# The value products of two attention stages and the steps up to their transposes, one slot later

## Reference

```
x = LN(x + window_attention(x))            # 16 heads of 8, window 16, token 0 attends to all
x = LN(x + causal_attention(x) + cross_attention(x, ctx))   # one output projection for the sum
x = LN(x + expert_choice_ffn(x))
x = LN(x + gated_recurrence_and_mlp(x))
x = LN(x + cross_attention(x, ctx))
x = LN(x + top2_of_8_experts(x))
```

## Time and profile before

| what | value |
|---|---|
| median of 3 runs | 590.47 us |
| profiled execution | 588.99 us |
| its span, first to last instruction | 587.3 us |
| around the span | 1.7 us |
| granted TensorE clock, mean | 0.946 |
| PE busy, share | 478.7 us, 82% |
| DVE busy, share | 381.4 us, 65% |
| ACT busy, share | 222.9 us, 38% |
| POOL busy, share | 181.0 us, 31% |

### The profile page before, as it was taken

How to read it: one execution, slowest core, us unless ns; L and a number is a source line. 1 busy time by engine, 2 the same in 40 slices (tenths; PEclk the granted TensorE clock), 3 DMA queues, 4 the chain that set the end, 5 groups by cost and what they waited for, 6 DMA issues and landing times. The chain is left out here.

```text
span 587.3 us, 10442 instructions
## 1 busy us (share of the span) xinstructions
PE 478.7 (82%) x3790; PEld 233.6 (40%) x3837; DVE 381.4 (65%) x876; ACT 222.9 (38%) x449; POOL 181.0 (31%) x296
## 2 busy tenths in 40 slices
PE   3899999978879889875079994697599888999994
PEld 2445444433334333332037992246333333444441
DVE  7454766877667686515996557954458875466474
ACT  2303444454746646651002102432202666724221
POOL 6651639457363370406200004300142400000000
PEclk9899999999989999997589997989599999999998
DMA  7230103055411120006212004000031200060700
GB/s 233 67 81 27 47 2 103 19 172 173 138 55 27 49 56 4 3 1 226 98 53 93 3 2 160 1 2 1 26 89 48 57 3 3 33 184 1 215 19 18
DMA packets 26899, 38.03 MB, mean 65 GB/s; under 512 B 3648, under 2 KB 19520, under 8 KB 26464
## 3 DMA queue, kind: packets, MB, share of 16 engines
q1 hardware_dynamic: 26848, 37.36, 21.0%
HBM read 23.91 MB, written 0.59 MB: 42 GB/s over the span
## 5 line engine op out<-in xcount | busy, mean ns | idle before, releaser
L1070 DVE TENSOR_REDUCE nmax<-bank 128x2 f32<-128x512 f32 (+2 forms) x240 | 144.9, 625 | 79.8 <-PE bank L844 34.1
L956 ACT ACTIVATE arena<-bank 128x512 f32<-128x512 f32 (+2 forms) x256 | 130.7, 526 | 121.7 <-PE bank L848 84.4
L502 PE MATMUL bank<-causal_qk,identb 128*128 128x512 bf16 x255 | 80.8, 418 | 33.6 <-DVE moe_top L1350 16.0
L844 PE MATMUL bank<-arena 62*128 62x256 bf16 (+2 forms) x512 | 86.0, 257 | 12.9 <-DVE nmax L1070 5.3
L848 PE MATMUL bank<-arena 64*128 64x256 bf16 (+2 forms) x512 | 85.6, 256 | 2.2 <-ACT arena L956 1.5
L889 PE MATMUL bank<-arena 128*32 128x256 f32 (+4 forms) x1088 | 72.8, 346 | 8.6 <-ACT arena L956 3.7
L844 PEld LDWEIGHTS bank<-arena 62*128 62x128 bf16 x512 | 29.9, 94 | 79.3 <-issue 46.0
L502 PEld LDWEIGHTS bank<-causal_qk,identb 128*128 128x128 bf16 x298 | 26.4, 105 | 68.4 <-issue 40.0
L714 POOL TENSOR_SCALAR_AFFINE_SELECT arena<-arena 128x256 f32<-128x256 f32 x64 | 25.5, 407 | 48.6 <-ACT arena L956 47.8
L848 PEld LDWEIGHTS bank<-arena 64*128 64x128 bf16 x512 | 30.3, 94 | 16.5 <-issue 6.9
L889 PEld LDWEIGHTS bank<-arena 128*32 128x32 f32 x1088 | 21.4, 109 | 33.7 <-issue 18.6
(11 more groups left out here) (284 smaller groups left out, 794.5 us busy)
## 6 DMA issues: line engine op xcount, KB each, us to landing
arena<-arena SPq DMA_DIRECT2D x96, 128.0 KB, 2.4
fcw<-in_fc1T SPq DMA_DIRECT2D x16, 256.0 KB, 3.3
arena<-in_fc2T SPq DMA_DIRECT2D x1, 4096.0 KB, 14.9
arena<-comb_rows SPq DMA_DIRECT2D x16, 256.0 KB, 4.7
fcw<-in_last SPq DMA_DIRECT2D x1, 2304.0 KB, 8.3
arena<-pos_rows SPq DMA_DIRECT2D x16, 128.0 KB, 3.0
arena<-comb_rows SPq DMA_DIRECT2D x16, 128.0 KB, 4.5
w<-in_w SPq DMA_DIRECT2D x1, 1216.0 KB, 6.1
```

What stands on the lines that cost most here:

```text
L502: nc.tensor.matmul(bank[:, :], m.identb[:, :], m.causal_qk[:, 0:4, :], start=True, stop=True)
L844: mins = t.matmul(mout[:, i, :], stack_rows(m, nm, h0 + i, 0, MAX_ROWS)[:, qt * P:(qt + 1) * P], stack_rows(m, nm, h0 + i, 1, MAX_ROWS)[:, ...
L956: s.activation(m.prob[h % 8][:, 0:w], score_bank(n, h)[:, 0:w], ACT.Exp).then_inc(exps, 1)
L1070: v.tensor_reduce(m.nmax[n % 2][:, qt, h0:h0 + nh], MX[c % NMX][:, 0:nh * (k1 - k0)].rearrange("p (h k) -> p h k", h=nh), AX.X, ALU.max, n ...
```

## The change

```
-S_EV = 57
+S_EV = 58
 Chain = namedtuple("Chain", "ott yt out norm x1t")
 OTT, YT, OUT, NORM, X1T = range(5)
-NEAR, FAR, LAST = Chain(59, 61, 63, 66, 67), Chain(60, 62, 65, 69, 71), Chain(60, 62, 64, 67, 68)
+NEAR, FAR, LAST = Chain(60, 62, 63, 66, 67), Chain(61, 63, 65, 69, 71), Chain(61, 63, 64, 67, 68)
...
-S_PV = 43
+S_PV = 44
```

## The result

The changed kernel takes 592.96 us (median of 20 runs, 589.66 to 601.33), the kernel before 590.90 beside it (20 runs). The ratio is 1.004, with a 95% interval of 1.0023 to 1.0058: slower, by about 2.4 us. One of the 20 runs, the 601.33, was in a slower state with a lower granted clock (0.926), and the ratio leaves it out. The forecast was 588.9, 1.6 faster. The measured time lies inside the stated range, but the change went the other way, and the small total hides gains and losses of 2 to 3 us each. The profiled execution took 595.46 us, with a span of 593.8.

A forecast was written before the change was run, and what follows sets the result against it. PE, in-order and busiest, was taken as the bound, with 8.6 us of product waits directly reachable. Terms -0.5 + 0.4 - 0.5 + 0.7 - 1.4 - 0.25 + 0 gave about -1.6: median 588.9 us, range 584.6 to 593.8.

The forecast's parts named there:

- So 0.51 becomes about 1.15: Cross job's start, layer 0: PE's wait for the exponential grows by 0.65 us, as L948 now stands ahead of it.
- -0.5 + 0.4: Layer 0's starts: three cross starts gain 0.5 us in all, three self starts lose 0.4.
- -1.4: Last job of layer 0: ACT stays fed because one more head is issued before the product; range -0.6 to -1.7 us.
- +0.7: NEAR, first job's output: L754 newly waits for copy L933, now behind an exponential; range 0 to +1.2 us.
- 4.9 for the quotients (L1020): Layer 0: PE's 4.9 us of waits for quotients, counted as unchanged because the distance between their steps stays the same.
- -0.5: LOCAL jobs: the product's 0.71 us wait goes, scores take back about 0.2; range 0 to -0.7 us.
- -0.25 (0 to -0.8): Layer 1: of 0.8 us of product waits, 0.55 belongs to the last group and stays, so 0.25 us is won.
- FAR keeps two slots and pays nothing: FAR jobs' output: unlike NEAR, L754 gets no new wait for copy L933; cost zero.
- zero: LAST, layer 1: L811's 0.59 us wait is covered, but L754 newly waits 0.5 to 0.6; zero in sum.
- L948 takes over: Rival, chance 0.13: the copy's new wait comes whole in seven places, mask waits only move along; +3.9, 594.4 us.
- The product waits go and nothing takes their place: Rival, chance 0.14: 7.4 us of product waits vanish without replacement; with NEAR -6.7, 583.8 us.
- The clock falls more often: Rival, chance 0.07: three more clock falls cost 3.6 us, giving 592.5 us; five give 594.9.

The follow-up runs named there:

- e8: Kernel before with only layer 0's self and cross jobs a slot later, but the copy L948 in its old slot: 595.08 us, ratio 1.008.
- e4: Kernel before with only layer 0's eight self and cross jobs a slot later, all four steps: 587.03 us, ratio 0.9945.
- e6: Kernel before with layer 1's four jobs a slot later and the router's weights on VectorE one slot later too: 590.43 us, single run.
- e9: Kernel before with products and copy a slot later in all jobs of both layers, chain (ott, yt) left in place: 587.21 us, ratio 0.9964.
- e10: Kernel before with products and copy a slot later in layer 0's self and cross jobs alone, chain left in place: 585.73 us, ratio 0.9924.
- e3: The whole change, with VectorE's quotients issued ahead of the mask of the same slot: 591.54 us, ratio 1.0032 against the kernel before.
- e7: Kernel before with only layer 0 a slot later and VectorE's quotients ahead of the mask of the same slot: 588.09 us, single run.
- e2: Kernel before with only layer 1's four jobs a slot later, layer 0 as before: 592.90 us, ratio 1.0039.
- e5: Kernel before with only the last job of layer 1 (LAST) a slot later: 592.6 us, single run.
- e1: Kernel before with only layer 0's twelve jobs a slot later, layer 1 as before: 590.46 us, ratio 1.000.

## Why the prediction was wrong

**Cross and self starts.** The step "So 0.51 becomes about 1.15" was right in size and place; that the copy L948 makes up 0.4 of it stays open (e8). At slot 108 PE waits 1.22, at the like places 0.75, 1.16, 0.75, 1.16 and 0.13, where 1.15 and 0.65 by turns were forecast. PE and ACT in after, the first cross start:

```profile
134.62 0.60 ACT L948 COPY ot<-bank 128x512 f32<-128x512 f32 x1
135.09 0.52 ACT L956 ACTIVATE arena<-bank 128x384 f32<-128x384 f32 x1
```

```profile
135.76 0.27 PE L844 MATMUL bank<-arena 62*128 62x256 bf16 x1 [1.22 <-ACT arena L956]
```

The exponential ends at 135.61 and PE goes on at 135.76. At 207.36 the label names the reduction L1070, which ended at 207.31, and the exponential at 207.21: the two came together. The mask waits went. The terms "-0.5 + 0.4" were too small: in e4, which moves only these jobs, slots 96 to 192 take 3.1 us less than before, of which 1.4 is a fall to 1.2 GHz that the kernel before had (128 to 144: 19.69, and 144 to 160: 17.63; in e6 without it 18.60 and 17.35). Against e6 they take 2.5 less. So it is about -2 (-1.7 to -2.5) instead of -0.1. In slots 96 to 112 of e4 the mask wait of 0.90 is gone and the wait for y is 0.33 instead of 0.90, which the prediction had at "0.9 to 1.0"; the rest wasn't followed wait by wait.

**The last job of layer 0.** "-1.4": slots 208 to 229 give -0.75, and 192 to 208 give back 0.45. ACT's gaps did go, yet -0.3 is left. With the chain left alone (e9, e10) these two stretches give -1.06 and -0.04. The self, cross and last jobs together are -2.0 to -2.8 for a forecast of -1.5: right in sign, and too small.

**NEAR.** "+0.7": the wait of the first L754 is there and is 0.90, and L766 waits 0.38 more (0.67 for 0.29). As a stretch, slots 54 to 64 cost 0.31, though they hold a half product less; against e9, which has the same work there and leaves the chain alone, they cost 0.62.

```profile
75.13 0.68 PE L754 MATMUL bank<-w,yT 128*128 128x128 f32 x4 [0.90 <-ACTq L935]
...
81.92 0.67 PE L766 MATMUL bank<-xT,h 128*128 128x256 f32 x2 [0.67 <-ACTq L942]
```

**The LOCAL jobs, the first step that failed.** The prediction set "4.9 for the quotients (L1020)" among the waits "between steps whose distance does not change". The distance between the transposes and their readers on PE didn't change; what stands between on VectorE did. In its place the runs showed 2.3 us of new waits in slots 64 to 96, shown by e3 and e7: the wait for y went from 0.36 to 1.07 and from none to 1.58. The term "-0.5" for these jobs was +0.9 and +1.5 in the two stretches. To be seen before: for the quotients' old and new slot the list of what VectorE does in it. The DMA wait behind it was foreseen and is real (1.34 in e7), but in the changed kernel the wait for y lay ahead of it, so there was none of "the DMA wait at slot 102 near 2 us".

**Layer 1, the second step that failed.** "-0.25 (0 to -0.8)" was +2.0 by stretches (-0.27 +0.52 +0.72 -0.04 +1.1 with e3's undisturbed end) and +2.5 by medians (e2). Only the product's waits were priced, 0.8 us in all; the chain's new place was put at nothing. e9 shows that the chain is the cause: with the products as late and the chain left alone, layer 1's stretches take 0.76 less than before, and with it 2.0 more. What the chain ran into, as far as it was followed: the quotients stood behind the router's weights (0.45, shown by e6); L754 waited 0.33 and 0.30 for the copy L933, against "FAR keeps two slots and pays nothing", and has no such wait in e9; and in slots 64 to 80 PE waits 2.31 us for VectorE's reductions instead of 1.69, but 1.42 in e9. So it isn't that PE lacks the product as work there. The wait of 0.30 at L1764 is also in e9, so it comes with the later product or its copy. LAST at "zero" was right (+0.1 by e5).

**The sum.** Self and cross about -2.0, last job -0.3, and layer 1 +2.0. The first four jobs are e1 less e4: without the stretches that the clock touched -0.23 (slots 38 to 54), +0.31, +0.92 (after less e4), +1.47, +0.50, -0.84, +0.23 and, up to slot 176, -0.53, which is +1.8, where the forecast had +0.2 (the parts from slot 96 on are the least sure, as alike traces differ there by up to 0.9). Together +1.5; measured +2.1 by medians. e4 and e1 say the same with the runs' own spread: -3.3, +3.4, and +2.5 for layer 1.

**The rivals.** "L948 takes over" named slower, but not this way: the mask waits did go, and the places that it named are in sum no loss. "The product waits go and nothing takes their place" did not come true in the changed kernel; e10 comes nearest to it, with L889's waits at 4.7. "The clock falls more often" isn't the cause of the shift. A long stretch at 1.2 GHz does stand in the profiled execution, just after the wait of 1.58 us:

```profile
117.10:130.80 13.70, 13.31 (x94) 5.44 (x95) 8.45 (x19) 3.93 (x10) 5.83 (x12) 0.50 0.57 174
```

(busy time by stretch, columns as in the earlier trace rows). Slots 80 to 112 took 43.5 us with it and 38.8 in e1 without, 4.7 of the 6.5 by which this execution is over the one before. But the mean granted clock over all runs is the same for both, 0.9405 (20 and 35 runs), e7, without the wait of 1.58, has a stretch as long (from 124.1, PEclk 0.50 over 13.7 us), and e1, with that wait, has none behind it (the granted clock was 1.00 from 117 to 131 us). The Trainium skill (TensorE: Matmul & The Clock Gate, "A second HAM failure mode: psum-queue depth-cycling") would have more short idles cost more clock. By these means they did not here, and in layer 0's slots 38 to 229 PE idles 17.8 us in e9 and 22.5 in e1, and e9 has the lower mean clock, 0.936 against 0.942.

## What to carry to other kernels

Where programs are in order, a step that is moved by one slot passes everything else in that slot on every engine that it touches, readers of its result included: list for the old and the new slot what stands ahead of it there and what that waits for. "The distance stays the same" is no argument for the engine in the middle. And try the producer alone first: here the later product won 0.4% in all jobs (e9) and 0.8% in the self and cross jobs alone (e10), and its chain, moved along with it, turned the 0.4% gain into a loss of the same size.

## What was not expected of the hardware

- **The spread of one kernel's runs goes with the clock.** Within each kernel a mean granted clock lower by 0.001 comes with 0.17 to 0.40 us more; the changed kernel took 589.66 us at 0.952 and 601.33 at 0.926. Compared at 0.942, before is at 590.2, after at 592.9 and e4 at 587.9.
- **Much of that spread arises where nothing was changed.** Between the two pipelines (from the last head of layer 0 to the first of layer 1) every trace has falls to 1.2 GHz, some of 13.7 to 20.5 us. That part took 192.8 to 196.6 us in the 14 traces, with 47.8 us of it at 1.2 GHz in the shortest and 61.4 in the longest. In layer 0's slots 38 to 229 the kernel before fell for 3.4 us at a time, and e3, e7 and after for 13.7.
- **The mask L1008 took 1.10 us** in the row at 114.46, and 0.73 and 0.76 for the same shape in the kernel before and in e3. In all 14 traces it took 0.44 to 0.46 us when GpSimd ran nothing beside it or only its own masks (L701 to L714), and it was longer, up to 1.29, only where a tensor_tensor or a copy of GpSimd (L673 to L684, L690) ran at the same time, as L673 did from 114.10 on. So part of the wait of 1.58 is the mask's own length beside GpSimd. No run moves GpSimd's work alone.
